# Head transfers in order of need, modulations in three pieces, statistics spread over slots, three VectorE steps dropped, light stages in another order

## What is computed

```python
mod = (silu(c) @ wmod)                 # 16 x (sa, ca, ga, sb, cb, gb), 128 each
ga, gb = sign(.) * max(|.|, 0.25)
h = layernorm(x) * (1 + ca) + sa
x = x + ga * causal_attention(h, W, b)
h = layernorm(x) * (1 + cb) + sb
light = attention in windows of 128 rows, 8 heads of 64, of rmsnorm(h)
scores_q, idx_q = route(h, q_tok, 128)     # 50 steps of coordinate descent, top 128
scores_kv       = route(h, kv_tok, 256)
heavy = 8-head attention of the chosen 128 rows over all 256, times scores
x = x + gb * (light + scatter(heavy, idx_q))
```

## Time and profile before

| | us |
|---|---|
| median of 3 runs | 502.33 |
| lowest and highest | 501.16, 502.41 |
| the profiled execution's own time | 501.88 |
| its span, first to last instruction | 500.1 |

### The profile page before, as it was taken

One profiled execution on the slowest core, in us unless ns is written; L12 is line 12 of the kernel. 1 busy time (PEld: TensorE's weight loads), 2 busy tenths in 40 slices (PEclk: granted clock), 3 DMA queues, 4 the chain that ended last, 5 costly groups with the idle time before them and its releaser, 6 DMA issues.

```text
span 500.1 us, 11927 instructions
## 1 busy us (share of the span) xinstructions
PE 447.7 (90%) x4021; PEld 390.7 (78%) x4021; DVE 346.6 (69%) x1130; ACT 346.5 (69%) x1260; POOL 263.8 (53%) x297
## 2 busy tenths in 40 slices
PE   3676888999899989988997989999999999999994
PEld 1464777888898977877886977889888889888883
DVE  6767788778788998789779984545546564556551
ACT  2268898778798868857776757767666777667761
POOL 7316566375566676331333334554555666655655
PEclk9999999999999999989999889999999999999998
DMA  8860000000001010000000000100010000110002
GB/s 223 252 263 23 13 11 12 12 23 23 12 22 32 5 32 23 22 12 2 12 13 10 12 2 18 33 17 7 11 18 13 12 12 11 17 18 11 7 7 21
DMA packets 18107, 16.26 MB, mean 33 GB/s; under 512 B 1952, under 2 KB 16816, under 8 KB 17792
## 3 DMA queue, kind: packets, MB, share of 16 engines
q1 hardware_dynamic: 14048, 11.70, 7.4%
q0 software_dynamic: 3248, 3.41, 4.2%
q10 hardware_dynamic: 752, 0.40, 0.3%
HBM read 10.23 MB, written 5.28 MB: 31 GB/s over the span
## 4 chain that ended last, share of the span: by engine, by line
PE 49%; DVE 11%; POOL 4%; issue 4%; ACT 3%; POOLq 0%; ACTq 0%; DVEq 0%
PE bank L872 6%; PE bank L883 5%; PE bank L898 5%; PE bank L780 4%; PE bank L639 4%; PE bank L641 4%; PE bank L640 4%; PE bank L810 4%; PE bank L839 3%; PE bank L910 3%; DVE cd_min L1182 2%; ACT pr L570 2%; PE bank L794 2%; POOL pr L399 2%; PE bank L821 2%
## 5 line engine op out<-in xcount | busy, mean ns | idle before, releaser
L399 POOL TENSOR_TENSOR pr<-pr,rinv 128x512 f32<-128x512 f32 x64 | 66.8, 1044 | 100.6 <-DVE rinv L1142 100.3
L411 POOL TENSOR_TENSOR pr<-pr,rinv 128x512 f32<-128x512 f32 x64 | 72.8, 1158 | 63.5 <-DVE rinv L1287 63.5
L570 ACT ACTIVATE pr<-bank,nmx 128x128 f32<-128x128 f32 x256 | 90.5, 378 | 20.1 <-DVE nmx L1136 20.1
L613 ACT ACTIVATE pr<-bank,nmx 128x256 f32<-128x256 f32 x128 | 59.5, 488 | 19.3 <-DVE nmx L1281 19.3
L1281 DVE TENSOR_REDUCE nmx<-bank 128x2 f32<-128x512 f32 x64 | 41.9, 682 | 35.0 <-PE bank L872 35.0
L623 ACT ACTIVATE pt<-bank 128x512 f32<-128x512 f32 x64 | 38.2, 597 | 27.5 <-PE bank L883 27.5
L570 ACT ACTIVATION_READ_ACCUMULATOR pr<-bank,nmx 128x1 f32 x256 | 55.8, 218 | 0.0
L794 PE MATMUL bank<-ident,pr 128*128 128x128 f32 x256 | 39.2, 275 | 11.6 <-POOL pr L399 9.8
L1136 DVE TENSOR_REDUCE nmx<-bank 128x4 f32<-128x512 f32 x64 | 42.3, 673 | 6.8 <-PE bank L780 6.6
L794 PEld LDWEIGHTS bank<-ident,pr 128*128 128x128 f32 x256 | 29.5, 140 | 17.8 <-POOL pr L399 12.4
L883 PE MATMUL bank<-ident,pr 128*128 128x128 f32 x256 | 38.9, 274 | 2.3 <-ACT pt L623 2.3
(11 more groups left out here) (222 smaller groups left out, 1318.7 us busy)
## 6 DMA issues: line engine op xcount, KB each, us to landing
mod_bc<-mod_rows_scratch SPq DMA_DIRECT2D x1, 3072.0 KB, 11.5
X<-in_L_attn_x SPq DMA_DIRECT2D x4, 512.0 KB, 9.0
xh_scratch<-xhs SPq DMA_DIRECT2D x16, 128.0 KB, 1.8
out<-X SPq DMA_DIRECT2D x16, 128.0 KB, 1.8
mod_bc<-mod_rows_scratch SPq DMA_DIRECT2D x1, 1024.0 KB, 4.5
wkv_raw<-in_L_ffn_wkv_light SPq DMA_DIRECT2D x1, 512.0 KB, 10.7
wmod_sb<-in_L_wmod ACTq DMA_DIRECT2D x1, 384.0 KB, 5.4
wq_raw<-in_L_ffn_wq_heavy POOLq DMA_DIRECT2D x1, 256.0 KB, 7.1
```

The lines of the kernel that those rows point to most:

```text
L399: pool.tensor_tensor(q, q, rinv[u][:, :, None].broadcast_to([P, 4, P]), ALU.mult)\
L411: pool.tensor_tensor(q, q, rinv[u][:, 0:2, None].broadcast_to([P, 2, N]), ALU.mult)\
L570: act.activation(pr[u][:, i * P:(i + 1) * P], ps[bank][:, i * P:(i + 1) * P], ACT.Exp, bias=nmx[u][:, i:i + 1], accum_out=sums[u][:, i:i + ...
L613: act.activation(pr[u][:, i * N:(i + 1) * N], ps[bank][:, i * N:(i + 1) * N], ACT.Exp, bias=nmx[u][:, i:i + 1], accum_out=sums[u][:, i:i + ...
```

## The change

- **Transfers.** SyncE now issues all loads, in another order: x piece 0, `w_at`, the row for `bv_bc`, x piece 1, the rows for `tok_bc`, light Q, K and V weights, the modulations' write, their first piece, the heavy weights, the second piece, the light output weight, x piece 2, the third piece, x piece 3, the heavy output weight. GpSimd issues no load. `bv_bc` and the heavy output weight have semaphores of their own.
- **Modulations** come back in three pieces: batch rows 0 and 1, 2 to 5, 6 to 15.
- **Statistics.** Only x piece 0 is done in the head; its bias is made for batch row 0 first, then for 1 to 3. Pieces 1 to 3 are done in slots 4, 11 and 19 (`late_stats`), their power one slot later (`late_rstd`), their bias two slots later.
- **Weights** are split in slots 3 (V), 4 (Q), 6 (K), 8 (KH), 10 (VH and QH).
- **Three VectorE steps go.** `mask_max` now writes the negated scores and their minimum, so that `neg_max_a` falls away and `exps_a` reads with scale -1. `var_eps` and `norm_squares` move to GpSimd, in front of the powers that use them.
- **Tables.** The A and L steps of all tables get other places and lags. The relative order of the H steps is the same on every engine.

The diff, without most of the tables:

```diff
-        MOD_FIRST = 4
+        MOD_PIECES = ((0, 2), (2, 6), (6, B))
+        MOD_AT = [lo for lo, _ in MOD_PIECES]
+        STAT_PIECES = ((0, 1), (1, 4), (4, 8), (8, 12), (12, 16))
         ROUNDS = NQ // 8
-        HEAVY_PIECES = (4, 6)
+        HEAVY_PIECES = (7, 9)
+        LIGHT_AT = (3, 4, 6)
+        STATS_AT = (4, 11, 19)
...
+            load_x(0)
+            sp.dma_start(w_at[:, :], w_attn).then_inc(w_at_in, 16)
+            load_row(bv_bc[:, :], b_attn[2 * D:3 * D], bv_in)
+            load_x(1)
+            load_row(tok_bc[:, 0, :], q_tok, bc_in)
+            load_row(tok_bc[:, 1, :], kv_tok, bc_in)
             sp.dma_start(wq_raw[:, 0, :], wq_l).then_inc(wl_in, 16)
             sp.dma_start(wkv_raw[:, :], wkv_l).then_inc(wl_in, 16)
-
-            for dst, src in ((bv_bc[:, :], b_attn[2 * D:3 * D]), (tok_bc[:, 0, :], q_tok), (tok_bc[:, 1, :], kv_tok)):
-                sp.dma_start(dst, src.rearrange("(a d) -> a d", a=1).broadcast_to([P, D])).then_inc(bc_in, 16)
...
+            spread_mod(0)
+            sp.dma_start(wq_raw[:, 1, :], wq_h).then_inc(wh_in, 16)
+            kv_rows = wkv_h.rearrange("(q i t m) d -> i t m q d", i=2, t=2, m=DH)
+            for i in range(2):
+                sp.dma_start(wk_hT[i * DH:(i + 1) * DH, :, :], kv_rows[i, 0]).then_inc(wh_in, 16)
+                sp.dma_start(wv_hT[i * DH:(i + 1) * DH, :, :], kv_rows[i, 1]).then_inc(wh_in, 16)
+            spread_mod(1)
+            sp.dma_start(wo_l_sb[:, :, :], wo_l.rearrange("(q p) d -> p q d", p=P)).then_inc(wo_in, 16)
+            load_x(2)
+            spread_mod(2)
+            load_x(3)
+            sp.dma_start(wo_h_sb[:, :, :], wo_h.rearrange("(q p) d -> p q d", p=P)).then_inc(woh_in, 16)
...
-                pool.dma_start(wv_hT[i * DH:(i + 1) * DH, :, :], kv_rows[i, 1]).then_inc(wh_in, 16)
-            pool.dma_start(wo_l_sb[:, :, :], wo_l.rearrange("(q p) d -> p q d", p=P)).then_inc(wo_in, 16)
-            pool.dma_start(wo_h_sb[:, :, :], wo_h.rearrange("(q p) d -> p q d", p=P)).then_inc(wo_in, 16)
-
-            rstd1(1, 4 * C, B * C)
+            rstd1(0)
+            rstd1(1)
+
+            def late_rstd(t):
+                if t - 1 in STATS_AT:
+                    rstd1(2 + STATS_AT.index(t - 1))
 
...
             def ln2_rstd(b):
+                pool.wait_ge(a["mv"], 2 * b + 2)
+                at_least(pool, a["hn"], 2 * (b - 1))
+                pool.tensor_scalar(ve2[b % 2][:, :], mv2[b % 2][:, :, 1], LN_EPS, None, ALU.add).then_inc(a["ve"], 1)
                 pool.wait_ge(a["ve"], b + 1)
-                at_least(pool, a["hn"], 2 * (b - 1))
                 pool.tensor_tensor(rs2[b % 2][:, :], ve2[b % 2][:, :], neg_half[:, 0:C], ALU.pow).then_inc(a["rs"], 1)
...
+                pool.wait_ge(a["ss"], 2 * b + 2)
+                at_least(pool, a["xh"], b - 1)
+                pool.tensor_scalar(ssc[b % 2][:, :], ss[b % 2][:, :], 1e-24, 1.0 / D, ALU.max, ALU.mult).then_inc(a["ssc"], 1)
                 pool.wait_ge(a["ssc"], b + 1)
-                at_least(pool, a["xh"], b - 1)
                 pool.tensor_tensor(rn[b % 2][:, :], ssc[b % 2][:, :], neg_half[:, 0:C], ALU.pow).then_inc(a["rn"], 1)
...
-                act.wait_ge(nm1_done, 1 if b < 4 else 2)
+                act.wait_ge(nm1_done, 1 if b == 0 else 2 + b // 4)
...
                 k = b % 2
-                act.wait_ge(a["nmx"], b + 1)
+                act.wait_ge(a["sm"], 2 * b + 2)
                 at_least(act, a["PTp"], b - 1)
                 at_least(act, a["ri"], b - 1)
-                act.activation(sm[k][:, 0:P], sm[k][:, 0:P], ACT.Exp, bias=nmxa[k][:, 0:1],
+                act.activation(sm[k][:, 0:P], sm[k][:, 0:P], ACT.Exp, bias=nmxa[k][:, 0:1], scale=-1.0,
                                accum_out=suma[k][:, 0:1]).then_inc(a["p"], 1)
-                act.activation(sm[k][:, P:3 * P], sm[k][:, P:3 * P], ACT.Exp, bias=nmxa[k][:, 1:2],
+                act.activation(sm[k][:, P:3 * P], sm[k][:, P:3 * P], ACT.Exp, bias=nmxa[k][:, 1:2], scale=-1.0,
                                accum_out=suma[k][:, 1:2]).then_inc(a["p"], 1)
...
-            run_slots([("H", 12, out_heavy), ("L", 2, project_q_l), ("L", 9, values), ("L", 8, p_transpose, 3),
...
+            run_slots([("L", 3, project_k_l), ("L", 8, p_transpose, 3), ("H", 12, out_heavy), ("A", 4, scores_a),
...
-            mean_var1(0, 0, 4)
-            stats1(1)
-            neg_mean_rstd(0, 0, 4)
+            mean_var1(0)
             dve.wait_ge(col_ps, 1)
             dve.tensor_copy(modT[:, 0, :], ps[7][:, 0:B]).then_inc(col_sb, 1)
             dve.tensor_scalar(modT[:, 1, :], ps[7][:, B:2 * B], 1.0, None, ALU.add).then_inc(col_sb, 1)
+            neg_mean_rstd(0)
...
-            stats1(2)
+            neg_mean_rstd(1)
...
-            split(V_w, wkv_raw[:, HID:2 * HID], gam_col[:, 0:1], 0)
-            dve.wait_ge(bc_in, 16 * 3)
-            dve.wait_ge(g_tab, 5)
-
             def weights(t):
 
-                if t == 1:
+                if t == LIGHT_AT[0]:
+                    dve.wait_ge(wl_in, 32)
+                    split(V_w, wkv_raw[:, HID:2 * HID], gam_col[:, 0:1], 0)
+                elif t == LIGHT_AT[1]:
                     dve.wait_ge(w_small, 2)
                     split(Q_w, wq_raw[:, 0, :], gam_sc[:, 0:1], 1)
-                elif t == 2:
+                elif t == LIGHT_AT[2]:
                     split(K_w, wkv_raw[:, 0:HID], gam_col[:, 0:1], 2)
-                elif t == 4:
-                    dve.wait_ge(wh_in, 80)
-                    dve.tensor_scalar(QH_w[:, :], wq_raw[:, 1, :], gam_sc[:, 1:2], None, ALU.mult).then_inc(w_scaled, 1)
-                elif t - 1 in HEAVY_PIECES:
+                if t - 1 in HEAVY_PIECES:
                     n = HEAVY_PIECES.index(t - 1)
                     dve.wait_ge(w_ps, n + 1)
                     split((KH_w, VH_w)[n], ps[7][:, :], gam_col[:, 1:2], 3 + n)
+                    if n == 1:
+                        dve.tensor_scalar(QH_w[:, :], wq_raw[:, 1, :], gam_sc[:, 1:2], None, ALU.mult).then_inc(w_scaled, 1)
+
+            def late_stats(t):
+                if t in STATS_AT:
+                    stats1(1 + STATS_AT.index(t))
+                    mean_var1(1 + STATS_AT.index(t))
...
-                    dve.tensor_tensor_reduce(sm[k][:, s:e], ps[a_bank("s", b)][:, s:e], mask[:, s:e], 1.0, -3.0e38, ALU.add, ALU.max,
-                                             mxa[k][:, i:i + 1]).then_inc(a["sm"], 1)
-
-            def neg_max_a(b):
-                k = b % 2
-                dve.wait_ge(a["sm"], 2 * b + 2)
-                dve.tensor_scalar(nmxa[k][:, :], mxa[k][:, :], -1.0, None, ALU.mult).then_inc(a["nmx"], 1)
+                    dve.tensor_tensor_reduce(sm[k][:, s:e], ps[a_bank("s", b)][:, s:e], mask[:, s:e], -1.0, 3.0e38, ALU.add, ALU.min,
+                                             nmxa[k][:, i:i + 1]).then_inc(a["sm"], 1)
...
-                if b in (0, MOD_FIRST):
-                    dve.wait_ge(mod_in[b // MOD_FIRST], 16)
+                if b in MOD_AT:
+                    dve.wait_ge(mod_in[MOD_AT.index(b)], 16)
...
+                at_least(dve, a["rs"], b - 1)
                 for i in range(C):
                     dve.bn_aggr(mv2[b % 2][:, i, :], st2[b % 2][:, i, :]).then_inc(a["mv"], 1)
...
-            def var_eps(b):
-                dve.wait_ge(a["mv"], 2 * b + 2)
-                at_least(dve, a["rs"], b - 1)
-                dve.tensor_scalar(ve2[b % 2][:, :], mv2[b % 2][:, :, 1], LN_EPS, None, ALU.add).then_inc(a["ve"], 1)
...
-            def norm_squares(b):
-                dve.wait_ge(a["ss"], 2 * b + 2)
-                at_least(dve, a["rn"], b - 1)
-                dve.tensor_scalar(ssc[b % 2][:, :], ss[b % 2][:, :], 1e-24, 1.0 / D, ALU.max, ALU.mult).then_inc(a["ssc"], 1)
-
```

126 lines of the change are left out of this document (63 added, 63 removed).

## The result

| | before | after |
|---|---|---|
| median, us | 502.37 | 485.99 |
| lowest and highest of four | 501.16, 502.50 | 484.62, 486.84 |
| span of the profiled execution, us | 500.1 | 485.0 |

The changed kernel takes 0.969 of the time before (95% interval 0.967 to 0.971), 16.4 us less.

A forecast was written before the change was run, and what follows sets the result against it. TensorE, busy 447.7 of 500.1 us, bounds the kernel, so only its idle or low-clock time can be won; VectorE's queue paces the front. 6.8 - 2.4 + 2.5 + 1.5 = 8.4 us gave 493.9 us, range 488.5 to 501.0.

The forecast's parts named there:

- The head until the masking: Start of the kernel: batch row 0's first masking starts at 16.6 us instead of 23.82, 7.2 us earlier.
- `ao` of batch row 0: End of the head: 9.0 us after the masking, at 25.6 instead of 32.41 us, 6.8 us earlier.
- Transfers: Head loads: modulations at most 0.4 us late, heavy weights 0 to 1.7 us; nothing charged for either.
- The fill: Until slot 14: VectorE's displaced work takes back 2.4 us of the lead, bounds 0 and 6.0.
- The joint stage: First and light attention together, to slot 50: 2.5 us won, a quarter of TensorE's waits; bounds 0 and 6.
- The late stage and the passage: Late light stage: wait for GpSimd's weights filled, lower clock avoided once, 1.5 us won; bounds -2 and +4.
- rival 3: GpSimd becomes late by its two new steps and delays p_transpose: 505.8 us, at worst 512.0; slower, mostly GpSimd, 0.10.
- Rival 2: More is won: the fill hides all, the joint stage gives 5 us, 489.0 us; chance 0.12.

The follow-up runs named there:

- Slot 13: Changed kernel with the statistics of x piece 2 in slot 13 instead of 11; 485.97 us.
- the kernel with the new order at 0.95: Changed kernel with x piece 2's statistics in slot 13 and ScalarE's `ln1` of batch rows 0 to 5 one slot later; 488.38 us.
- Head: Kernel before with only the new transfers, modulations in three pieces, and statistics and weight splits in slots; 505.97 us, ratio 1.011.
- steps: Kernel before with only the three VectorE steps taken off, old transfers and old order tables; 497.95 us, ratio 0.994.
- head and steps: Changed kernel with the old order tables, the three new statistics calls put in; 504.09 us, ratio 1.007.
- steps and order: Changed kernel with the transfers, two modulation pieces, statistics and weight splits of the kernel before; 494.79 us, ratio 0.987.
- head and order: Changed kernel with all three dropped steps back on VectorE; 500.06 us, ratio 0.997.

## Why the prediction was wrong, point by point

- **The head until the masking: right, in part by luck.** The masking came at 16.73 (forecast 16.6), 7.1 us earlier (7.2), because the first scores end at 16.69 (16.6). The V split started at 13.07 (13.3), but not when `wkv_raw` landed: that was issued at 5.1 and took 6.9 us, so it was there at 12.0. VectorE's own queue held the split until 13.07. The transfer was 1.3 us quicker than my 13.3, and it made no difference.
- **`ao` of batch row 0: 5.1 us earlier, not 6.8.** From masking to `ao` it took 10.55 us instead of 9.0. Row 0's exponentials end at 18.6, but its p_transpose starts at 23.08 on TensorE, behind row 1's scores. I had followed row 0's chain and not what the new order puts in front of it.
- **Transfers: right, nothing to charge.** No `ao` of the fill waited for a modulation, and the heavy weights were there when TensorE transposed them at 27.01. The estimate that I drew from *DMA: Bandwidth & Descriptors* of the Trainium skill, "Anatomy of one DMA", 2.1 us for the write, is nearer to the 1.6 us of the emptied queue than the 8.4 of the full one. The page fits its formula to transfers issued by GpSimd; I used it for one of SyncE's.
- **The fill: the loss was the whole 5 us, not 2.4.** At light scores 0 the lead is 0.1 us in the profiled execution. My step counted VectorE's displaced work and let its pauses hide a third. What happened is that TensorE waits 4.0 us in one piece and then works at the lower clock. Slot 13 takes away 2.5 us of this wait, and a wait for `kT` and the clock take the gain back. TensorE is busy for 36.94 of the 57.02 us up to scores 0; a lead in such a stretch is not a sum of VectorE steps.
- **The joint stage: 7.8 us instead of 2.5, beyond the bound of 6.** This is the first failed term. I had taken a quarter of TensorE's 9.6 us of waits as what VectorE's relief would give, and the new order as a risk. The steps without the new order give 1.5 us here. With the order, idle time falls to 1.6 us in 117.84. But the order with the three steps on VectorE takes 127.90 us, 2.3 more than before: the gain needs both. What the two bring together had no term in my sum: I looked at what becomes adjacent, and not at whether a period has a wait left at all. The order alone, with the old head and the steps kept, was not run.
- **The late stage and the passage: 6.2 us instead of 1.5, beyond the bound of 4.** This is the second failed term. I had the wait as "filled rather than shortened", with VectorE setting the length of a period and the lower clock as all that there was to win, once. The clock did go from 0.95 to 1.00 from scores 12 to 17, with scores at 2.06 us behind each wait shown, but the kernel with the new order at 0.95 shows that this is worth only 1.8 of the 5.2 us there. The other 3.4 are shorter periods, at which I had put nothing; TensorE's waits for GpSimd's weights fell from 5.1 to 3.4 us in this stage. I gave no price to the periods in which light and heavy work overlap. The swap that I described is needed for this gain; that it carries it alone is not shown.
- **GpSimd (rival 3): out.** Its new steps take 0.23 us, a third of the bound of 0.71, and doubling them costs at most 0.8 us. *GPSIMD Engine Reference* of the Trainium skill, "Elementwise — side-by-side cycle accounting", speaks for VectorE on the duration of such work. The traces agree: the median is 226 and 234 ns on GpSimd against 170 and 156 on VectorE, whose means of 268 and 237 hold a few steps of up to 0.70 us. But here the place in the queue decides: the step that waits for ScalarE's squares costs 10.5 us on VectorE.
- **The terms were added; they do not add.** Head +4.7, steps -3.3, head and steps +2.9, steps and order -6.4, head and order -1.5, all three -16.4 us (each against the runs of before beside it). Rival 2 ("more is won", 489.0) was nearest, by luck: its sum has 6.8 us from a head whose lead did not last, and 5 and 1.5 us for stages that gave 7.8 and 6.2.

## What to carry to other kernels

A small step that waits for another engine should stand where its queue comes to it late enough: on the engine that uses its result, or a slot later if its users can wait (here they couldn't: 514.63 us). In VectorE's queue, one slot too early, it stopped the evacuations of everything else. Price a new order by what idle time is left in a whole period, with the period's full idle time to start from and not a share of the waits by name (7.2 us from scores 1 to 8, of which 5.6 were won, and 2.1 of busy time besides), and price the lower clock beside it, but not by its busy time: 3.0 us more of TensorE's busy time at 0.95 cost 1.8 us of the stage here. A lead won ahead of a stretch in which the bounding engine often idles is worth nothing until it is seen behind that stretch.

## What I had not expected of the hardware

- Several short waits can cost more clock than a long one: after 4.00 us of waiting TensorE ran at 0.66 from 40 to 45 us and was back at 1.00; after waits of 1.48, 0.59, 1.67 and 0.54 us it ran at 0.50 for the whole of 45 to 50 us, while busy all the time.
- The same 32 KB write took 8.4 us with ten loads in front of it in its queue and seven issued by GpSimd, and 1.6 us with eight in front and none by GpSimd. Which of the two queues held it up is not shown.
- In the kernel with the doubled steps, 32 more GpSimd steps of 0.23 us, 7.4 us of busy time, moved the end by less than 1 us, though GpSimd's weights are among the last things that TensorE waits for.
